# Ternary FFN on eight cores: five w2 tiles loaded ahead of the last blocks of the second product's input

## The chip, the cores and the metric

One Trainium2 chip, eight cores on two dies (cores 0 to 3, cores 4 to 7). Each core computes one eighth of the rows (half of one batch entry, 2048 of 4096 positions) of the same program, on its own data and with the same weights. The time is that of the slowest core, in microseconds (us) on the device. The kernel before took 2494.3 us as the median of three runs (2493.86, 2494.3 and 2610.59).

## The reference, cut to what matters

```python
x = _layernorm(x + attention(x, Wq, Wk, Wv, Wo))          # linear attention, 16 heads, 4 kv heads
# FFN with ternary weights:
def absmean_quant(w):
    scale = jnp.mean(jnp.abs(w))
    mask = (jnp.abs(w) >= scale * 0.7).astype(w.dtype)
    return jnp.sign(w) * mask                             # -1, 0 or 1
h = jnp.einsum('bsd,fd->bsf', x, absmean_quant(w1)) + b1  # 2048 -> 8192
h = jax.nn.gelu(h)
out = jnp.einsum('bsf,df->bsd', h, absmean_quant(w2)) + b2  # 8192 -> 2048
x = _layernorm(x + out)
```

x is (4, 4096, 2048) in f32, w1 is (8192, 2048), w2 is (2048, 8192). Both thresholds need the mean of the whole weight matrix before its first element can be made ternary.

## The kernel before, in words

Each core runs, in this order: keys, values and the small key-value matrices for a batch entry; queries and the attention output; the output projection with the first layer norm; the first FFN product (lines 742 to 828; the input in two halves P of 1024 rows, 64 steps u = 2j + P, each giving two blocks of 128 hidden features; from u = 4 each by seven block products in place of eight, Strassen's way); and the second FFN product (lines 830 to 874).

**The change to the second product** is the place of this case. The hidden activations h are bf16. They are written by ScalarE after the gelu (`store_hid`, line 1241) to a DRAM buffer `hd` in pieces of 256 KB, since on-chip memory has no room for them beside the first product's operands. For the second product they are read back by the SyncE queue (SP): `load_hid(P, half, a, b, signal)`, lines 409 to 412. P says which 1024 rows, half which 512 of them, a to b which of the 64 feature blocks (128 KB each). What is waited for before a piece may be loaded is the store of its last blocks (`d_hs`), and the end of the products or evictions that still use the memory under it.

The second product has passes: s is which 1024 rows, g which 512 of the 2048 output columns, and P (this loop's own name for the half) which 512 rows. In a pass TensorE goes through 16 weight tiles q of 2048 x 128 elements, 16 matmuls of 128x512 for each tile (4 blocks fc = 4q + j by 4 row chunks cc), 256 in all (line 856). Pass (s 0, g 0, P 0) is called the first pass below, (s 0, g 0, P 1) the second pass. The first one uses half 0 of the input, the second one half 1, with the same 16 weight tiles.

**The weight tiles** of w2 come in f32, 1024 KB each, into one of three stages, by `load_w2(r)`, lines 452 to 462, r = 16g + q. VectorE makes each ternary in two instructions (lines 960 and 963, `tern_w2` and `ternary`) and writes it as fp8, so that TensorE may use it (line 837 waits for `v_w2`). Tiles 0 to 6 of g 0 are made during the first product, and kept in MB (`W2_PRE = 7`). From tile 7 on the three stages are used in turn (MA's first half, MA's second half, MC), so the load of tile r waits for the ternary tile r - 3 to be done: `e.wait_ge(v_w2, r - 2)`, line 456. GpSimd stores each ternary tile to DRAM (`store_w2`, line 589, 256 KB), from where the second 1024 rows read it.

**What sets the order here** is the SP program, written out by hand: SP waits for semaphores in its order, and a DMA behind a wait isn't issued before that wait is over. The DMAs that SP has issued run on its own hardware queue (q1 on the page); ScalarE's (`store_hid`, and `load_x1r` for the residual) run on q10, GpSimd's on q0, all on the same 16 DMA engines. At the change of products SP does, in lines 472 to 492: load tiles 7 and 8; load half 0 blocks 0 to 12, 12 to 36; tile 9; blocks 36 to 60; wait until the stores of the other 1024 rows have landed (`d_hs[2]`, `d_hs[3]`, lines 482 and 483), since blocks 60 to 64 overwrite the memory from which they are sent; blocks 60 to 64; wait for the last eviction and gelu of the first product and for the stores of half 1; then four times a tile and 16 blocks of half 1; then the other tiles. TensorE waits for half 0 at q 0, 3, 9 and 15 (line 840), and for half 1 at q 0, 4, 8 and 12 of the second pass (line 842).

After a pass VectorE adds each of the four PSUM banks to a piece of the residual (line 1098), and GpSimd stores it.

Of the kernel before, what the change touches and what calls it, by code (L numbers as in the profile page):

```python
# [80 lines left out]
W2_PRE = 7  # L81


def build_nc():
# [191 lines left out]
    def hid_rows(a, b, half):  # L276
        base, o = (r1, (24576 + a * 512) if a < 12 else (a - 12) * 512 if a < 60 else 30720) if half == 0 else (
            (rw, a * 512) if a < 32 else (r3, 16384 + (a - 32) * 512))
        return base[:, o:o + (b - a) * 512]
# [50 lines left out]
    def n_m(u, i):  # L330
        return 7 * (u - NU_CL) + i
# [16 lines left out]
    def n_hs(j):  # L348
        return 16 * (j + 1)
# [3 lines left out]
    def n_qs(j, i):  # L353
        return 5 * (j - NU_CL // 2) + i
# [28 lines left out]
    def w2_stage(r):  # L383
        if r < W2_PRE:
            return w2_slot7
        j = (r - W2_PRE) % 3
        return maf[:, j * 2048:(j + 1) * 2048] if j < 2 else mcf[:, 0:2048]

    def w2_signal(r):
        return d_s7 if r < W2_PRE else (d_st[0], d_st[1], d_mc)[(r - W2_PRE) % 3]  # L390
# [12 lines left out]
    def sync_program(e):  # L403
# [5 lines left out]
        def load_hid(P, half, a, b, signal):  # L409
            e.wait_ge(d_hs[2 * P + half], n_hs((b - 1) // 2))  # L410
            e.dma_start(out=hid_rows(a, b, half),
                        in_=hd[P, half, :, a * 512:b * 512]).then_inc(signal, 16)
# [39 lines left out]
        def load_w2(r):  # L452
            if r == 0:
                e.wait_ge(d_x1[2], 16 * 5)
            elif r < W2_PRE or r >= W2_PRE + 3:
                e.wait_ge(v_w2, r if r < W2_PRE else r - 2)
            elif r < W2_PRE + 2:
                e.wait_ge(v_w1, 63 + r - W2_PRE)
            else:
                e.wait_ge(t_m, n_m(63, M3))  # L460
                e.wait_ge(p_q, n_qs(31, Q2))
            e.dma_start(out=w2_stage(r), in_=w2h[r // 16, r % 16]).then_inc(w2_signal(r), 16)
# [16 lines left out]
        e.wait_ge(t_m, n_m(63, M3))  # L479
        load_w2(W2_PRE + 2)  # L480
        load_hid(0, 0, 36, 60, d_ha[2])
        e.wait_ge(d_hs[2], n_hs(31))
        e.wait_ge(d_hs[3], n_hs(31))
        load_hid(0, 0, 60, 64, d_ha[3])
# [1 line left out]
        e.wait_ge(a_h, n_h(63, H22))  # L486
        e.wait_ge(d_hs[1], n_hs(31))
        for i in range(4):
            load_w2(W2_PRE + 3 + i)
            load_hid(0, 1, 16 * i, 16 * i + 16, d_hb[i])  # L490
        for r in range(W2_PRE + 7, 64):
            load_w2(r)

        e.wait_ge(t_z, 28)
# [839 lines left out]
    with nc.Block() as block:  # L1334
        block.sync(sync_program)
        block.gpsimd(gpsimd_program)
        block.vector(vector_program)
        block.scalar(scalar_program)
        block.tensor(tensor_program)
# [57 lines left out]
```

## Time and profile before

| | us |
|---|---|
| median of three runs | 2494.3 |
| the profiled execution | 2497.7 |
| its span on the slowest core (core 6) | 2496.2 |
| the spans of all eight cores | 2480.4 to 2496.2 |
| TensorE busy in that span | 2406.0 (96%) |
| VectorE, ScalarE, GpSimd busy | 1246.5, 725.6, 551.4 |
| chain that ended last: TensorE / DMA / VectorE | 87% / 10% / 2% |

How to read it: the page's busy share of TensorE says how much is left over all. Where the rest is can be read from a table of stretches with the granted clock (1.00 is the full 2.4 GHz) and from the idle times before TensorE's groups. A queue's rows (SPq) have the time at which a DMA was issued, and a DMA's landing is read from the listing of issues, which gives the time from issue to landing.

### The profile page before, as it was taken

The page shows a single profiled execution, that of the slowest core. Times are in us where ns is not written, and L with a number is a line of the kernel's source. Part 1 is how long each engine was busy: PE and PEld are TensorE (multiplying, and loading weights), DVE is VectorE, ACT ScalarE, POOL GpSimd, SP SyncE. Part 2 cuts the span into 40 slices and gives each one's busy share as a digit, 9 for nine tenths or more (in the row PEclk, how much of TensorE's full clock was granted, in tenths as well). Part 3 has the DMA queues.
Part 4 walks back from the last instruction along what each step waited for, and adds up shares of the span by engine and source line. Part 5 has one row for each costly group of instructions (what it writes and reads, how often), then busy time and mean ns, then how long its engine had stood idle before and what let it go on. Part 6 is the DMA issues. An engine that isn't in the chain of part 4 may idle for free.

```text
span 2496.2 us, 31950 instructions; the slowest of 8 cores (2480.4 to 2496.2 us)
## 1 busy us (share of the span) xinstructions
PE 2406.0 (96%) x11300; PEld 1094.4 (44%) x11300; DVE 1246.5 (50%) x1395; ACT 725.6 (29%) x1109; POOL 551.4 (22%) x419
## 2 busy tenths in 40 slices
PE   4999999999999999999999999799999999799997
PEld 1444444444444444444444444344444444344443
DVE  1222344445567777777788886375747211200021
ACT  0233477743323666666433333000000000000000
POOL 3000000004336334344343433011212000100000
PEclk9999999999999999999999999899999999899999
DMA  9994688696655887787544446976848577522253
GB/s 159 217 239 153 157 203 204 165 268 241 232 223 181 265 263 254 258 265 265 188 144 165 160 144 234 327 243 216 277 151 287 180 254 238 173 68 68 85 194 118
DMA packets 106955, 507.01 MB, mean 203 GB/s; under 512 B 12976, under 2 KB 12976, under 8 KB 69808
## 3 DMA queue, kind: packets, MB, share of 16 engines
q1 hardware_dynamic: 50400, 323.55, 38.9%
q0 software_dynamic: 27600, 124.80, 19.1%
q10 hardware_dynamic: 28800, 56.64, 7.3%
q8 instruction: 93, 1.52, 0.2%
q14 instruction: 62, 0.51, 0.1%
HBM read 444.11 MB, written 98.57 MB: 217 GB/s over the span
## 4 chain that ended last, share of the span: by engine, by line
PE 87%; DMA 10%; DVE 2%; issue 1%; POOL 0%; ACT 0%; SPq 0%; DVEq 0%; POOLq 0%; ACTq 0%
PE PB L767 29%; PE PB L856 25%; PE PB L694 8%; PE PB L731 8%; PE PB L870 4%; PE PB L668 4%; PE PB L658 4%; PE PB L758 2%; DMA MA<-w2h 2%; DMA out<-MA 2%; DMA R<-woh 2%; DMA RW<-wvh 2%; DMA zs<-MC 1%; DMA MC<-x1s 1%; DMA hd<-R 1%
## 5 line engine op out<-in xcount | busy, mean ns | idle before, releaser
L856 PE MATMUL PB<-R 128*128 128x512 fp8e4 x2576 | 572.2, 385 | 34.2 <-DVE MC L1098 17.9
L767 PE MATMUL PB<-R,RW 128*128 128x512 bf16 x2400 | 537.6, 379 | 0.0
L856 PEld LDWEIGHTS PB<-R 128*128 128x128 bf16 x2576 | 254.6, 99 | 350.5 <-issue 55.4
L767 PEld LDWEIGHTS PB<-R,RW 128*128 128x128 fp8e4 x2400 | 234.7, 98 | 283.0
L579 POOL TENSOR_TENSOR RW<-MC 128x1024 fp8e4<-128x1024 fp8e4 x120 | 244.1, 2066 | 283.1 <-DVE MC L963 283.1
L1098 DVE TENSOR_TENSOR MC<-PB,MC 128x512 f32<-128x512 f32 x56 | 38.4, 685 | 404.6 <-PE PB L856 243.9
L694 PE MATMUL PB<-R,MB 128*128 128x512 bf16 x1024 | 231.1, 379 | 0.0
L767 PE MATMUL PB<-R,MC 128*128 128x512 bf16 x960 | 226.8, 379 | 0.0
L856 PE MATMUL PB<-R,RW 128*128 128x512 fp8e4 x784 | 170.4, 379 | 0.0
L960 DVE TENSOR_SCALAR MB<-MA,thr 128x2048 fp8e4<-128x2048 f32 x102 | 137.8, 1351 | 54.6 <-DMA MA<-w2h 40.9
L963 DVE SCALAR_TENSOR_TENSOR MC<-MA,thr,MB 128x2048 fp8e4<-128x2048 f32 x64 | 158.3, 2473 | 7.0 <-DVE MB L960 0.5
L694 PEld LDWEIGHTS PB<-R,MB 128*128 128x128 bf16 x1024 | 100.1, 98 | 120.7
L658 PE MATMUL PB<-RW,R 128*128 128x512 bf16 x512 | 121.2, 390 | 28.1 <-DMA R<-xb 28.1
L1225 ACT ACT_TABLE_LOAD x1 | 1.3, 1283 | 503.1 <-DVE mv L1106 503.1
L767 PEld LDWEIGHTS PB<-R,MC 128*128 128x128 fp8e4 x960 | 93.9, 98 | 113.3
L597 POOL DMA_DIRECT2D zs<-MC x56 | 35.3, 630 | 448.9 <-DVE MC L1098 446.1
L1153 ACT ACTIVATE MA<-MA 128x2048 f32<-128x2048 f32 x69 | 130.8, 1895 | 9.8 <-DMA MA<-w1h 9.7
L1272 ACT ACTIVATE RW<-PB 128x512 f32<-128x512 f32 x180 | 105.2, 594 | 90.2 <-PE PB L767 88.3
L1324 ACT ACTIVATE lnv<-mv,c_eps_ln 128x1 f32<-128x1 f32 x8 | 2.4, 294 | 424.1 <-DVE mv L1142 416.9
L668 PE MATMUL PB<-RW,R 128*128 128x512 bf16 x512 | 119.5, 387 | 5.8 <-DMA RW<-wvh 5.8
L1253 ACT ACTIVATE R<-RW,b_sb 128x512 bf16<-128x512 f32 x120 | 85.8, 719 | 129.6 <-DVE RW L1083 62.9
L1253 ACT ACTIVATE RW<-RW,b_sb 128x512 bf16<-128x512 f32 x120 | 86.0, 720 | 127.6 <-DVE RW L1083 64.8
(134 smaller groups left out, 2525.6 us busy)
## 6 DMA issues: line engine op xcount, KB each, us to landing
MA<-w1h SPq DMA_DIRECT2D x126, 1024.0 KB, 6.5
MB<-w2h SPq DMA_DIRECT2D x108, 512.0 KB, 7.8
MA<-w2h SPq DMA_DIRECT2D x45, 1024.0 KB, 7.8
MC<-w2h SPq DMA_DIRECT2D x19, 1024.0 KB, 7.8
R<-xb POOLq DMA_DIRECT2D x32, 512.0 KB, 78.5
x1s<-R POOLq DMA_DIRECT2D x16, 1024.0 KB, 4.6
hd<-RW ACTq DMA_DIRECT2D x64, 256.0 KB, 4.6
hd<-R ACTq DMA_DIRECT2D x64, 256.0 KB, 4.9
```

Of the source, the lines that this page charges most:

```text
L579: e.tensor_tensor(w_sum(j, k), x, y, op, saturate=False).then_inc(p_q)
L658: ins = e.matmul(PB[sc % 2], xs(blk % 4, dc)[:, cc * 128:(cc + 1) * 128], wk_sb(dc), start=(dc == 0), stop=(dc == 15))
L668: ins = e.matmul(PB[2 + sc % 2], xs(blk % 4, dc)[:, cc * 128:(cc + 1) * 128], wv_sb(dc), start=(dc == 0), stop=(dc == 15))
L694: ins = e.matmul(PB[n % 3], wq_sb(ic)[:, dc * 128:(dc + 1) * 128], x_own(t, dc), start=(dc == 0), stop=(dc == 15))
L731: ins = e.matmul(PB[WO_BANK[i % 4]], attn_chunk(c, ic), wo_sb(ic, g), start=(ic == 0), stop=(ic == 15))
L767: ins = e.matmul(PB[m_bank(u, i)], w[:, dc * 128:(dc + 1) * 128], x[:, dc * 512:(dc + 1) * 512], start=(dc == 0), stop=(dc == 7))
L856: ins = e.matmul(PB[F2_BANK[P][cc]], hid(fc, P)[:, cc * 128:(cc + 1) * 128], w2q_sb(s, g, q)[:, j * 512:(j + 1) * 512], start=(fc == 0), s ...
L960: e.tensor_single_scalar(b8t, src, thr[:, 2 * no:2 * no + 1], ALU.is_le, saturate=False).then_inc(v_b)
L963: e.scalar_tensor_tensor(dst, src, thr[:, 2 * no + 1:2 * no + 2], b8t, ALU.is_ge, ALU.subtract, saturate=False).then_inc(signal)
L1153: e.activation(stage(j), stage(j), AF.Abs, accum_out=wsum[:, i:i + 1]).then_inc(a_abs)
L1253: e.activation(hb(P, half, par), src, AF.Gelu, bias=b1_sb[:, 2 * j + par:2 * j + par + 1]).then_inc(a_h)
L1272: e.activation(tq(u, slot), PB[m_bank(u, i)], AF.Copy).then_inc(a_c)
```

## The change

SP's order in the change of products. Tiles 10 to 14 are issued right behind blocks 36 to 60 of half 0, ahead of the waits for the stores and of blocks 60 to 64. Then blocks 60 to 64, and then four times 16 blocks of half 1 and a tile (15 to 18), the blocks ahead of the tile. Tiles 19 to 63 are as before. No other engine's program is changed, nor any wait on another engine.

```diff
@@ -479,6 +479,9 @@
         e.wait_ge(t_m, n_m(63, M3))
         load_w2(W2_PRE + 2)
         load_hid(0, 0, 36, 60, d_ha[2])
+
+        for r in range(W2_PRE + 3, 15):
+            load_w2(r)
         e.wait_ge(d_hs[2], n_hs(31))
         e.wait_ge(d_hs[3], n_hs(31))
         load_hid(0, 0, 60, 64, d_ha[3])
@@ -486,9 +489,9 @@
         e.wait_ge(a_h, n_h(63, H22))
         e.wait_ge(d_hs[1], n_hs(31))
         for i in range(4):
-            load_w2(W2_PRE + 3 + i)
             load_hid(0, 1, 16 * i, 16 * i + 16, d_hb[i])
-        for r in range(W2_PRE + 7, 64):
+            load_w2(15 + i)
+        for r in range(19, 64):
             load_w2(r)
```

The SP queue at this place, from blocks 36 to 60 of half 0 (the first row, 128x12288) to the third piece of half 1. `w2h` are the f32 weights, `hd` the hidden activations; 128x2048 from `hd` is blocks 60 to 64, 128x8192 is 16 blocks of half 1.

```order
 L411 DMA R<-hd 128x12288
+L462 DMA MA<-w2h 128x2048 x2
+L462 DMA MC<-w2h 128x2048
+L462 DMA MA<-w2h 128x2048 x2
 L411 DMA R<-hd 128x2048
-L462 DMA MA<-w2h 128x2048
+L411 DMA RW<-hd 128x8192
+L462 DMA MC<-w2h 128x2048
 L411 DMA RW<-hd 128x8192
 L462 DMA MA<-w2h 128x2048
-L411 DMA RW<-hd 128x8192
-L462 DMA MC<-w2h 128x2048
```

Five tile loads (10 to 14) now stand ahead of the short piece of half 0. Tile 15 (into MC) has now blocks 60 to 64 and one piece of half 1 ahead of it; it had all four pieces of half 1 and tiles 10 to 14 ahead of it before.

## Rows read from the trace of the kernel before

**Rows 1.** Stretches of core 6: engines' busy us (instructions), clock, DMA share, GB/s.
```profile
1550.00:1633.10 83.10, 66.85 (x258) 27.30 (x257) 34.28 (x21) 1.54 (x3) 6.07 (x9) 0.84 0.96 315
1633.10:2019.00 385.90, 385.90 (x1790) 174.94 (x1789) 211.33 (x152) 0.00 (x0) 63.81 (x76) 1.00 0.69 224
```

**Rows 2.** TensorE in order of time: start, us, what, idle before and releaser.
```profile
1550.05 24.34 PE L856 MATMUL PB<-MB,R 128*128 128x512 fp8e4 x112
1574.22 13.98 PE L856 MATMUL PB<-R 128*128 128x512 fp8e4 x64
1592.28 6.50 PE L856 MATMUL PB<-R 128*128 128x512 fp8e4 x16 [4.08 <-DVE R L963]
...
1613.17 6.30 PE L856 MATMUL PB<-R 128*128 128x512 fp8e4 x16 [3.91 <-DVE R L963]
1623.53 9.70 PE L856 MATMUL PB<-R 128*128 128x512 fp8e4 x32 [4.05 <-DVE R L963]
1633.06 24.34 PE L856 MATMUL PB<-MB,RW 128*128 128x512 fp8e4 x112
```

**Rows 3.** VectorE in order of time: second instruction of tiles 7, 9, 10 and 11.
```profile
1552.91 2.35 DVE L963 SCALAR_TENSOR_TENSOR R<-MA,thr,MB 128x2048 fp8e4<-128x2048 f32 x1
...
1560.61 2.35 DVE L963 SCALAR_TENSOR_TENSOR R<-MC,thr,MB 128x2048 fp8e4<-128x2048 f32 x1
...
1580.30 2.35 DVE L963 SCALAR_TENSOR_TENSOR R<-MA,thr,MB 128x2048 fp8e4<-128x2048 f32 x1
...
1589.79 2.35 DVE L963 SCALAR_TENSOR_TENSOR R<-MA,thr,MB 128x2048 fp8e4<-128x2048 f32 x1
```

**Rows 4.** The SP queue in order of time (issues).
```profile
1550.83 20.50 SPq L411 DMA_DIRECT2D R<-hd  x2
1571.59 0.61 SPq L462 DMA_DIRECT2D MA<-w2h  x1
1572.30 0.43 SPq L411 DMA_DIRECT2D RW<-hd  x1
...
1592.21 0.33 SPq L462 DMA_DIRECT2D MA<-w2h  x1
```

**Rows 5.** The SP queue's own waits, 1500 to 1665: total, times, longest.
```profile
SPq L483 <- DMA hd<-R: 12.9, 1, 12.9
```

**Rows 6.** Single issues: KB, us to landing. Issued 1550.39, 1550.83, 1571.59, 1572.30, 1592.21.
```profile
MC<-w2h SPq DMA_DIRECT2D x1, 1024.0 KB, 7.7
R<-hd SPq DMA_DIRECT2D x1, 3072.0 KB, 19.9
MA<-w2h SPq DMA_DIRECT2D x1, 1024.0 KB, 7.2
RW<-hd SPq DMA_DIRECT2D x1, 2048.0 KB, 13.2
MA<-w2h SPq DMA_DIRECT2D x1, 1024.0 KB, 27.3
```

**Rows 7.** Two short stretches of the first pass (columns of rows 1).
```profile
1585.00:1590.00 5.00, 3.20 (x15) 1.26 (x13) 1.50 (x2) 0.00 (x0) 0.00 (x0) 1.00 1.00 369
1590.00:1600.00 10.00, 6.50 (x16) 2.15 (x16) 3.03 (x2) 0.00 (x0) 0.54 (x1) 0.66 1.03 340
```

**Rows 8.** TensorE behind a wait of 3 us: core 6, then core 1 (x208 each).
```profile
776.81 46.13 PE L758 MATMUL PB<-R,MC 128*128 128x512 bf16 x208
769.43 45.06 PE L758 MATMUL PB<-R,MC 128*128 128x512 bf16 x208
```

**Rows 9.** All TensorE waits of core 6: total, times, longest.
```profile
PE PB L856 <- DVE MC L1098: 17.9, 4, 10.8
PE PB L856 <- DVE R L963: 16.2, 4, 4.2
```

**Rows 10.** Spans and clocks of the two slowest cores.
```profile
core 0: 2491.5 us, clock 0.989
...
core 6: 2496.2 us, clock 0.987
```

## The prediction, made before the changed kernel ran

> **What bounds the kernel now.** I read the stretches first: around the change of products TensorE's clock is at a mean of 0.84 and TensorE is busy 66.85 of 83.1 us, while the next 386 us are busy throughout at 1.00 [rows 1]. So the whole of what this edit can touch is in the first pass of the second product. TensorE in order of time gives the size: the first pass starts at 1550.05 and the second at 1633.06, 83.0 us apart. 112 matmuls without a gap take 1574.22 - 1550.05 = 24.17 us from start to start, 0.2158 each, so 256 would take 55.25 [rows 2]. The pass loses 27.8 us. The same rows say how: the tiles up to 10 come in time, and each of tiles 11 to 14 is waited for by about 4 us, released by the second ternary instruction. The four waits are 16.2 us in all [rows 9]. Behind each the 16 matmuls take 6.3 to 6.5 us in place of 3.62 (three times, about 8.2 us) and the last 32 take 9.70 in place of 7.07 (2.6) [rows 2]: they run in part at 1.2 GHz, mean clock 0.66 in the ten microseconds behind the first wait [rows 7]. 16.2 + 8.2 + 2.6 = 27.0; the other 0.8 is starting up again.
>
> What is late is the transfer. VectorE needs 3.8 us for a tile (1552.91 to 1560.61 for two tiles [rows 3]), but tile 10 is only ready at 1582.65 and tile 11 at 1592.14. Tile 10's stage was free at 1555.26, when tile 7 was done [rows 3]; its load was issued at 1571.59 [rows 4], since SP stood in front of it for the last of the activation stores, 12.9 us of it on one wait [rows 5]. From there tiles and pieces of half 1 alternate, so each tile carries 2048 KB that nobody needs before the second pass. The issue-to-landing rows give the rate: half 1's first piece lands at 1572.30 + 13.2 = 1585.5, tile 14 at 1592.21 + 27.3 = 1619.5, and between these lie 10 MiB (tiles 11 to 14 and three pieces), 3.40 us for one MiB [rows 6].
>
> **The change, step by step** (times of core 6).
>
> 1. *Blocks 36 to 60* are issued and land as before: 1550.83 + 19.9 = 1570.7 [rows 6]. TensorE wants them at tile 9, at 1550.05 + 9 x 3.45 = 1581.1. The new loads stand behind them in the same queue.
>
> 2. *Tiles 10, 11, 12* are issued at 1555.3, 1559.1 and 1563.0, when tiles 7, 8 and 9 are done [rows 3]. They run behind the piece, by the rate above landing at 1574.1, 1577.5 and 1580.9. Made ternary with 3.8 us each: ready at 1577.9, 1581.7, 1585.5. TensorE would start tile 11 at 1550.05 + 11 x 3.453 = 1588.0 and tile 12 at 1591.5.
>
> 3. *Tiles 13 and 14* are issued when 10 and 11 are ready, 1577.9 and 1581.7. The queue still has work then. They land at about 1584.3 and at 1588 to 1589 (the latter by 7.2 us from issue, as tile 10 had [rows 6]), ready at 1589.3 and 1592.8; wanted at 1594.9 and 1598.4. All four waits of today go, 27.8 us with their slow matmuls.
>
> 4. *What is late next* is tile 15. In front of it now stand blocks 60 to 64 (0.5 MiB) and half 1's first piece (2 MiB). SP issues these behind load 14 at 1582 (the stores that it waits for had landed by 1570.9 before), and tile 15 when tile 12 is done, 1585.5. From 1570.7 on the queue has to move 5 tiles, 0.5 and 2 MiB and tile 15: 8.5 MiB at 3.40 = 28.9 us, so it lands at 1599.6, and is ready at 1603.4 + 0.1 for the handover. It is wanted at 1550.05 + 15 x 3.453 = 1601.85. That is a wait of 1.6 us. The rate may move either way: it was taken beside four stores of ternary tiles in 34 us, and now five or six fall into 25 us, which takes some of it; the engines moved 340 to 369 GB/s in all at this time [rows 7], and with 45 GB/s for the stores 295 to 325 GB/s are left, 3.55 to 3.23 us for one MiB, a wait of 0.2 to 2.9. I take 2.
>
> 5. *The clock behind that wait.* Nothing before shows a wait of 2 us here. The lower bound is nothing, as after a wait of 3 us on core 1 (208 matmuls in 45.06), the upper the 2.8 us that followed the waits of 4 us [rows 2]. The same 3 us on core 6 cost 46.13 - 45.06 = 1.07 in that row [rows 8]. I take 1.1, the nearest.
>
> 6. *Half 1 comes later*: its first piece at 1570.7 + 7.5 x 3.40 = 1596.2 in place of 1585.5. The second pass would start at 1550.05 + 55.25 + 3.1 = 1608.4, and wants one piece every 13.8 us. The others land behind tiles 15, 16 and 17, one every 10.2 us: about 1606, 1617 and 1627, against 1622, 1636 and 1650. Cost nothing, with a cover of 12 us or more. If that cover goes, each microsecond counts in full.
>
> 7. *Tiles 16 to 18* now land at 1610, 1620 and 1630, each behind a piece. They are wanted from 1608.4 + 55.25 = 1663.6 on, and from 19 on the loads go by the stages as before. Cost nothing; the cover is 30 us. SP's five moved issues cost 0.3 to 0.6 us each [rows 4] in time that it spent waiting. GpSimd's stores of ternary tiles follow the tiles and nobody waits for them here.
>
> Sum: -27.8 + 2.0 + 1.1 = -24.7 us. Everything behind the second pass is paced by TensorE or follows it, so it moves along. The profiled execution took 2497.7, so it would take 2473.0; the median of the runs is 3.4 lower, 2494.3, and gives 2469.6, **2470 us**. Core 6 is slowest by 4.7 us over core 0 [rows 10]; the edit takes about the same from each, so I let it stay.
>
> At step 4 a page speaks against my wait. The rate in the rows is 1048576 / 3.40 = 308 GB/s for SP's queue, and 340 and 369 for all queues. The Trainium skill's page "DMA: Bandwidth & Descriptors" (Specifications) gives about 358 GB/s as one core's share of HBM. An estimate from that page: 8.9 MB would take 24.9 us if SP's queue had all of it, tile 15 would land at 1595.6 and TensorE would not wait at all; the sum would be -27.8. The two rows lie on both sides of the page's figure, and they hold stores too.
>
> **The rivals.**
>
> *No wait at tile 15* (chance 0.18). If the queue moves one MiB in under 3.2 us, tile 15 is ready in time. The first piece of half 1 took 1585.5 - 1578.8 = 6.7 us for 2 MiB behind tile 10 [rows 6], 3.35 for one, which speaks for a rate near the edge. Time: 2494.3 - 27.8 = 2466.5. That is also where the page's figure above would put it.
>
> *Tile 15 much later* (0.16). Between tile 9's landing (1550.39 + 7.7 = 1558.1) and 1570.7 the queue needed 12.6 us for 3 MiB, 4.2 for one [rows 6], with the activation stores and the residual's loads beside it. At that rate 8.5 MiB take 35.7, tile 15 is ready at 1610.3, the wait is 8.4, and 2.8 go to the clock: -16.6, 2477.7. Against it: those stores and loads are over by then.
>
> *The gain is partly given back later* (0.06). Core 6 waits 17.9 us on evictions in the second half of the kernel [rows 9]. This follows from DMAs that start when TensorE ends its first 1024 rows, so it should only move; but a shift could change it by some 5 us either way: 2465 to 2475, or up to 2480 together with a later tile 15.
>
> *Slower than before* (0.02). Half 1's pieces, put behind five tiles, come too late for the second pass. It decides from 1608 on: the first piece would have to land after 1608.4 before anything is lost, and after 1633 before all the gain is. It has 2494.3 + (landing - 1633) as its time, 2497 if it lands at 1636. That would be 65 us for 7.5 MiB, 8.7 for one, twice the worst rate in the rows. SP's wait for the stores of half 1 could hold it up so, but the longest such wait was 12.9 us [rows 5].
>
> That leaves 0.58 for the forecast with gains of 22 to 27 (2467 to 2472). The low end is the first rival with 2.5 us for the scatter of the cores, 2464. The high end takes in the late tile 15 with some given back later, 2481. A change of 2% is 50 us (about what a measurement of this kernel tells from none), and the whole of what the first pass loses is 27.8. So within 2% has 0.97, faster 0.01, slower 0.02 for what no row shows.
>
> **What would show it.** In the changed kernel's trace: no wait of TensorE on the ternary instruction at tiles 11 to 14; the first pass 55 to 61 us long in place of 83.0; one wait of 0 to 4 us ahead of its last 16 matmuls; the tile loads of 10, 11 and 12 issued 3.8 us apart ahead of 1565; the first piece of half 1 landing ahead of the second pass; the clock over the first pass at 0.95 or more. It is wrong if tiles 11 to 14 are still waited for (the loads in front are slower than I read), if the second pass waits for half 1, or if the first pass is 25 us shorter and the span is not.

## The result, and the profile after

The changed kernel took 2474.35 us (median of four runs, 2472.83 to 2476.28). Its ratio to the kernel before is 0.9922, 95% interval 0.9902 to 0.9941: 19.5 us less of 2494.1. In some executions a whole die is disturbed and slower (two of the four now on record for the kernel before, 2610.59 and 2820.3); all ratios, and the medians below, leave these out. The forecast was 2470 and 24.7 us less. The profiled execution took 2473.52 us, its slowest core is core 6 again, with 2472.0 us in place of 2496.2; as a mean over the eight cores the span went from 2486.1 to 2467.0 us, 19.0 less. Run again on another chip it gave 0.9933 (0.9916 to 0.9950).

The stretches of core 6 of the changed kernel around the first pass, with the columns of [rows 1]:

```profile
1547.40:1612.90 65.50, 58.25 (x259) 25.66 (x257) 34.29 (x21) 1.55 (x3) 7.59 (x9) 0.92 0.99 307
1612.90:1990.00 377.10, 377.10 (x1749) 171.00 (x1748) 211.29 (x152) 0.00 (x0) 63.28 (x76) 1.00 0.74 243
```

TensorE of core 6 in order of time, the answer to [rows 2]:

```profile
1547.46 24.34 PE L859 MATMUL PB<-MB,R 128*128 128x512 fp8e4 x112
1571.63 27.79 PE L859 MATMUL PB<-R 128*128 128x512 fp8e4 x128
1606.67 6.36 PE L859 MATMUL PB<-R 128*128 128x512 fp8e4 x16 [7.25 <-DVE R L966]
1612.87 24.34 PE L859 MATMUL PB<-MB,RW 128*128 128x512 fp8e4 x112
```

The four waits at tiles 11 to 14 are gone: 112 + 128 matmuls run without a gap. One wait is there, 7.25 us ahead of the last 16 matmuls, and these take 6.36 us, 2.74 more than the 3.62 at 2.4 GHz: the mean clock of the pass is 0.92, and was 0.84. The first pass is 65.4 us long in place of 83.0. Over the eight cores its mean went from 81.6 to 64.2, and that is 17.5 us.

VectorE of core 6, the first ternary instruction of tiles 10, 11, 14 and 15; the SP queue; and the landing of the load of tile 15, issued at 1584.99 (answers to [rows 3, 4, 6]):

```profile
1573.13 1.29 DVE L963 TENSOR_SCALAR MB<-MA,thr 128x2048 fp8e4<-128x2048 f32 x1 [12.76 <-DMA MA<-w2h]
1577.32 1.29 DVE L963 TENSOR_SCALAR MB<-MA,thr 128x2048 fp8e4<-128x2048 f32 x1 [0.45 <-DMA MA<-w2h]
...
1588.87 1.29 DVE L963 TENSOR_SCALAR MB<-MA,thr 128x2048 fp8e4<-128x2048 f32 x1
1602.67 1.29 DVE L963 TENSOR_SCALAR MB<-MC,thr 128x2048 fp8e4<-128x2048 f32 x1 [10.06 <-DMA MC<-w2h]
```

```profile
1552.74 4.18 SPq L462 DMA_DIRECT2D MA<-w2h  x2
1560.44 0.33 SPq L462 DMA_DIRECT2D MC<-w2h  x1
1576.94 4.52 SPq L462 DMA_DIRECT2D MA<-w2h  x2
```

```profile
MC<-w2h SPq DMA_DIRECT2D x1, 1024.0 KB, 17.5
```

Tiles 10 to 14 come at the pace of VectorE, 3.85 us apart (4.19 between the first two, with 0.45 of waiting). Then it idles 10.06 us for tile 15, which landed at 1584.99 + 17.5 = 1602.5, 55.0 us after the pass began. The forecast had it at 49.55.

The TensorE waits of core 6, with [rows 9] as the lines of before:

```profile
PE PB L859 <- DVE MC L1101: 13.8, 2, 11.6
PE PB L859 <- DVE R L966: 7.2, 1, 7.2
```

Core 6's span is 24.2 us shorter, and that is 17.6 in the first pass, 4.1 less wait between the halves of the rows (17.9 to 13.8), and 2.6 by a first pass that began at 1547.46 in place of 1550.05. The last two are within the scatter of the cores and runs: over the eight cores the wait between the halves is a mean of 15.4 us before, 13.9 after, and 14.6 in the changed kernel run again, and the first pass begins 0.2 us earlier as a mean. So it is luck that core 6's 24.2 us come so near to the 24.7 of the forecast; the edit's own part is 17.5.

### The profile page after: what moved, and what is told of

The parts are those of the page before. It is cut to its first block, busy times and chain, and to the rows that moved or that the text cites. A ratio compares the mean times of both kernels' runs of the same rounds, so it can differ in the third digit from the quotient of the medians.

```text
span 2472.0 us, 31808 instructions; the slowest of 8 cores (2462.5 to 2472.0 us)
## 1 busy us (share of the span) xinstructions
PE 2388.4 (97%) x11158; PEld 1092.8 (44%) x11300; DVE 1246.5 (50%) x1395; ACT 725.9 (29%) x1109; POOL 553.9 (22%) x419
## 4 chain that ended last, share of the span: by engine, by line
PE 85%; DMA 10%; DVE 3%; issue 2%; POOL 1%; DVEq 0%; ACT 0%; POOLq 0%; ACTq 0%; SPq 0%
PE PB L770 29%; PE PB L859 25%; PE PB L697 8%; PE PB L734 7%; PE PB L873 4%; PE PB L661 4%; PE PB L671 4%; PE PB L761 2%; DMA R<-woh 2%; DMA RW<-wvh 2%; DMA out<-MA 1%; DMA zs<-MC 1%; DMA MA<-w2h 1%; DMA MC<-x1s 1%; DMA MA<-zs 1%
## 5 line engine op out<-in xcount | busy, mean ns | idle before, releaser
L859 PE MATMUL PB<-R 128*128 128x512 fp8e4 x2576 | 563.7, 382 | 21.1 <-DVE MC L1101 13.8
```

The source lines that it names most:

```text
L859: ins = e.matmul(PB[F2_BANK[P][cc]], hid(fc, P)[:, cc * 128:(cc + 1) * 128], w2q_sb(s, g, q)[:, j * 512:(j + 1) * 512], start=(fc == 0), s ...
```

## The experiments

What was open: why tile 15 is 5.4 us later than worked out, and where the cover of 12 and 30 us that steps 6 and 7 counted on stands. In the comparisons "start" is VectorE's first instruction of a tile, from the beginning of the first pass, as a mean over the eight cores. The changed kernel has tile 10 at 24.9 and tile 15 at 54.4, and in its repeat 25.5 and 54.9. "Mean span" is the mean over the eight cores and the runs, against the kernel before run beside it; the changed kernel's repeat has 17.4 us less.

**Tile 15 ahead of its piece.**

```diff
         for i in range(4):
-            load_hid(0, 1, 16 * i, 16 * i + 16, d_hb[i])
             load_w2(15 + i)
+            load_hid(0, 1, 16 * i, 16 * i + 16, d_hb[i])
```

> The changed kernel, but each of tiles 15 to 18 is issued ahead of its piece of half 1 and not behind it, so that only blocks 60 to 64 stand ahead of tile 15; tiles 10 to 14 stay early. In the changed kernel tile 15 landed 55.1 us after the first pass began, and the 2 MiB piece ahead of it took 8.1 us of the queue. Theory Q (tile 15 is late because of the bytes ahead of it in SP's queue): tile 15 is issued at 37.5, lands at 47 to 48, is ready at 51 to 52, wanted at 51.8: wait 0 to 0.5 us, first pass 55.3 to 56, second pass starts with a wait of 0 to 1 us for its first piece, which now lands at 55.4; 9 to 10 us faster than the changed kernel, about 0.988 of the kernel before (2465). Rival P (the piece is what the second pass can't spare): the second pass waits for pieces, 3 us or more, and under half of the 10 us stays. Rival W (tile 15 is late because SP waits for the store semaphores or for a stage): tile 15 still lands after 52, wait over 4 us.

Measured: tile 15's start is 47.4, the pass 55.2 to 57.3 us (mean 56.0, 8.1 less than in the changed kernel), the second pass waits 0.3 us for a piece on one core and nothing on the others. But the kernel has 0.9911 of before (0.9887 to 0.9935), median 2468.46: beside the 0.9922 of the changed kernel that is some 3 us and not 9 to 10, though both intervals are 5 us wide to either side. The mean span is 23.8 us less than before, so the mean core did get about 6 of the 8.1 us; the slowest core, which sets the time, did not. TensorE on core 2, which was the slowest:

```profile
1542.47 24.34 PE L859 MATMUL PB<-MB,R 128*128 128x512 fp8e4 x112
1566.64 27.79 PE L859 MATMUL PB<-R 128*128 128x512 fp8e4 x128
1595.61 3.61 PE L859 MATMUL PB<-R 128*128 128x512 fp8e4 x16 [1.17 <-DVE R L966]
...
1701.52 11.86 PE L859 MATMUL PB<-R 128*128 128x512 fp8e4 x48 [5.45 <-DVE R L966]
```

So theory Q holds for the first pass, P and W fall. And there is a wait that was not foreseen: 5.45 us at 1701.5, tile 12 of the third pass (the first with new weight tiles). All eight cores together give a mean of 2.0 us of such waits (0 to 5.9), which is about what the mean span lacks of the 8.1. VectorE shows why:

```profile
1600.15 0.67 DVE L1101 TENSOR_TENSOR MC<-PB,MC 128x512 f32<-128x512 f32 x1
...
1624.48 0.69 DVE L1101 TENSOR_TENSOR MC<-PB,MC 128x512 f32<-128x512 f32 x1 [22.85 <-DMA MC<-x1s]
...
1629.64 0.69 DVE L1101 TENSOR_TENSOR MC<-PB,MC 128x512 f32<-128x512 f32 x1 [3.67 <-DMA MC<-x1s]
...
1694.19 0.69 DVE L1101 TENSOR_TENSOR MC<-PB,MC 128x512 f32<-128x512 f32 x1 [10.56 <-DMA MC<-x1s]
```

Behind the first pass it stands 22.85 and 3.67 us in front of the residual for evictions 2 and 3, and only then makes tile 16; behind the second pass 10.56 us more, with tile 28 (tile 12 of the third pass) next in its program. Tile 16 starts 85.4 us after the first pass began, as a mean, and 89.8 in the changed kernel: VectorE's chain moved by 4.4 us where TensorE's moved by 8.1.

**The stores of the ternary tiles 7 to 15 held until tile 15 is ternary** (changed kernel otherwise; GpSimd's program).

```diff
         for q in range(16):
+            if q == 7:
+                e.wait_ge(v_w2, 16)
             store_w2(0, q)
```

> The changed kernel, but GpSimd stores the ternary tiles 7 to 15 only when tile 15 is ternary, so that none of these 256 KB stores runs beside SP's queue in the last 34 us before tile 15. Nothing is left out. In that stretch SP's queue had 82% of the DMA engines' time and the stores 11.5% (before: 92.6% and 7.4% in the stretch from which the rate of 3.40 us for one MiB was taken). Theory S (the stores share the engines): SP's share goes to 93%, the rate from 3.97 to about 3.5 us for one MiB, tile 15 lands at 51 to 52 us from the start of the first pass in place of 55.2, the wait falls from 7.25 to 3 to 4 us and the pass from 65.4 to about 61.5; time about 0.9905 of before. Rival C (the limit is the memory that all cores share, reads above all, and not the engines' time): SP's queue gets nothing, tile 15 lands at 54 to 56, wait 6.5 to 8. If deferring the stores costs something later (tile 16 may not be written before tile 7 to 15's stores have landed), it is seen as waits at tile 16, expected none.

Measured: tile 15's start is 49.2 (46.4 to 51.9) in place of 54.4, and tile 10's 23.3 in place of 24.9. Three cores have no wait at tile 15 at all, the others 1.1 to 4.0; the mean pass is 58.1 us. Rival C falls: SP's queue does get what the stores leave. The DMA queues of core 6 between the starts of tiles 10 and 15, the changed kernel first (29.5 us), then this one (24.8 us):

```profile
q1 hardware_dynamic: 988, 7.96, 84.4%
q0 software_dynamic: 400, 1.31, 11.0%
q10 hardware_dynamic: 117, 0.20, 3.0%
```

```profile
q1 hardware_dynamic: 996, 8.09, 96.1%
q10 hardware_dynamic: 118, 0.21, 3.2%
```

For about the same 8 MB SP's queue (q1) needed 29.5 us with 84.4% of the engines' time and 24.8 us with 96.1%: 269 and 326 GB/s, or 3.89 and 3.21 us for one MiB. The share alone makes 29.5 into 25.9 us (times 84.4 over 96.1). The other 1.1 us is that SP's own bytes took the engines 6% less time each without the stores beside them; why, no run here tells.

The time, 0.9920 of before (0.9897 to 0.9942), is that of the changed kernel all the same, and so is the mean span, 17.8 us less. On all cores TensorE now waits in the third pass from tile 12 on, 2.3 to 5.8 us in all (mean 4.1, of 6.0 won in the first pass). The expectation had none of that. Part of it is of the experiment's own making: GpSimd issues the nine held stores right ahead of the store of eviction 0, and VectorE stands 25.2 to 29.1 us in front of eviction 2, 18.3 to 20.1 in the changed kernel. Core 6:

```profile
1565.38 31.24 PE L861 MATMUL PB<-R 128*128 128x512 fp8e4 x144
...
1697.94 16.49 PE L861 MATMUL PB<-R 128*128 128x512 fp8e4 x64 [4.63 <-DVE R L968]
```

**The first residual loads held too.** In `load_x1r`, for the first one, `e.wait_ge(v_w2, 16)` on ScalarE's queue is added to the kernel above.

> As e2_stores_late, and the first loads of the residual (ScalarE's queue, 256 KB each, 2 KB packets) are also held until tile 15 is ternary. Theory S: another 5% of the engines' time for SP, tile 15 lands at 49 to 50.5 us from the start of the first pass, wait 1 to 2.5 us, pass about 59. Blocks 36 to 60 should also land a little earlier than 21.4. Rival C: no change against e2_stores_late. The evictions behind the first pass come later (about 20 us), which nobody should wait for.

Measured: tile 10 starts at 21.6, tile 15 at 47.3, the pass is 55.9 us as a mean: another 1.9 us, as theory S has it. The wait at tile 12 of the third pass is 4.0 to 13.0 us, on all cores, a mean of 7.0 of the 8.3 that the first pass won, and the one run took 2473.66 us.

**Pieces of half 1 ahead of the tiles alone**, in the kernel before.

```diff
         for i in range(4):
-            load_w2(W2_PRE + 3 + i)
             load_hid(0, 1, 16 * i, 16 * i + 16, d_hb[i])
+            load_w2(W2_PRE + 3 + i)
```

> The kernel before with one part of the change alone: each of the four pieces of half 1 is issued ahead of the tile with which it alternates (10 to 13), and no tile is moved up. Theory Q (bytes ahead in SP's queue set when a tile is there): tile 10 lands at about 36 us from the start of the first pass in place of 28.8, and each tile up to 13 about 7 us later than before, tile 14 and 15 by about nothing to 4; a new wait at tile 10 (wanted at 34.5, ready at 40), and the pass 83 to 88 us, so 0 to 5 us slower than before: 2494 to 2499. Rival: the order within the pairs makes no difference, pass 83 as before, no wait at tile 10.

Measured: tile 10 starts at 34.7 in place of 27.7, the 7 us of one piece, and is waited for on core 6 (5.49 us). The pass is 81.2 us as a mean, before 81.6; one run took 2487.96 us beside a kernel before of 2489.6. The order in the queue does what theory Q says, but the new wait at tile 10 takes the place of another: the queue has the same bytes to move until tile 14. I had expected up to 5 us more. By itself this half of the change brings nothing that one run can show, and within the change it costs the first pass 8 us (the first experiment).

**VectorE's order of evictions and tiles**, with tile 15 ahead of its piece. In each pass of the first 1024 rows three ternary tiles are put between the first two and the last two evictions; GpSimd's stores are put in the same order.

```diff
-        for c in range(4):
-            evict_z(0, 0, c)
         for g in range(4):
+            for c in range(2):
+                evict_z(0, g, c)
             if g < 3:
-                for q in range(12):
+                for q in range(3):
                     tern_w2(g + 1, q)
-            for c in range(4, 8):
+            for c in range(2, 4):
+                evict_z(0, g, c)
+            ...                     # tiles 3 to 11
+            for c in range(4, 6):
                 evict_z(0, g, c)
+            ...                     # tiles 12 to 14, evictions 6 and 7, tile 15
```

> e1_tile15_first, and VectorE (with GpSimd's stores in the same order) no longer waits idle for the residual between evictions 2 and 3 of a pass: three ternary tiles stand between the first two and the last two evictions of each pass of the first 1024 rows. In e1_tile15_first the eight cores waited up to 7 us in all (0 to 5.4 at once, about 152 us after the first pass began, which is tile 12 of the third pass), since VectorE had stood 17 to 26 us in front of two residual loads and then began tile 16 late. Theory G (the gain of a shorter first pass is given back there, because VectorE's chain of tiles 16 to 31 does not move with TensorE): these waits fall to 0 to 1 us, the mean over cores to under 0.3, all else as e1_tile15_first; about 0.9885 of the kernel before. Rival N (e1_tile15_first was held by other things, such as the evictions between the two halves of the rows or the spread between runs): the waits at 152 us go and the time stays at 0.991. Rival T (tiles 16 to 18 land late behind the pieces of half 1, so that moving them up in VectorE's order gives nothing): waits at 150 to 170 us stay.

Measured: 0.9887 of the kernel before (0.9871 to 0.9902), median 2462.68 us. The slowest core of the profiled run has 2461.1 us. The waits in the third pass are 0.55 and 0.90 us on two cores and none on the others, a mean of 0.18 in place of 2.0; the second pass starts with a wait of 0.3 and 0.8 us on two cores. This is theory G, and T falls. Against N stand the mean span, 26.5 us less than before, which is 9.1 less than the change on the same chip and about what its shorter first pass (55.8 for 64.4) gives, and the ratio beside the 0.9911 of the first experiment. That kernel ran on another chip, and the two intervals overlap, so how much the new order alone brings is not shown.

On VectorE of core 4, which was that slowest one, evictions 1 and 2 (line 1108, counted from 0) have now three tiles between them, and there is no wait for the residual:

```profile
1601.01 0.67 DVE L1108 TENSOR_TENSOR MC<-PB,MC 128x512 f32<-128x512 f32 x1
...
1606.49 1.29 DVE L970 TENSOR_SCALAR MB<-MA,thr 128x2048 fp8e4<-128x2048 f32 x1 [4.01 <-DMA w2qd<-R]
...
1618.73 1.29 DVE L970 TENSOR_SCALAR MB<-MA,thr 128x2048 fp8e4<-128x2048 f32 x1 [8.50 <-DMA MA<-w2h]
...
1632.05 1.28 DVE L970 TENSOR_SCALAR MB<-MC,thr 128x2048 fp8e4<-128x2048 f32 x1 [9.58 <-DMA MC<-w2h]
...
1635.71 0.68 DVE L1108 TENSOR_TENSOR MC<-PB,MC 128x512 f32<-128x512 f32 x1
```

It is the fastest kernel of this study; the change has 0.9933 on the same chip.

**The same order of VectorE with the change's order of SP.**

> The changed kernel with VectorE's and GpSimd's order of e5_tile15_first_evict_split alone; SP's order is the change's. The changed kernel has no wait at tile 12 of the third pass. Theory G: it is the cover that was used up, not yet a wait, so nothing moves: first pass 62 to 66 us as in the changed kernel with one wait at tile 15, time within 0.1% of the changed kernel beside it. Rival: the evictions or their order matter in themselves (in later passes, or between the halves), and it is 0.2% or more off.

Measured: 0.9925 (0.9909 to 0.9941), the change beside it 0.9933 (0.9916 to 0.9950); one wait at tile 15, 3.1 to 9.2 us, none in the third pass; the mean span is 18.1 us less than before, the change's 17.4. As expected: by itself the order of VectorE brings nothing that can be told here, since the change has no wait in the third pass.

**Half 1 in pieces of 4 blocks**, four DMAs in place of one, so rows of 4 KB and not of 16 KB.

> The changed kernel, each 16-block piece of half 1 loaded as four DMAs of 4 blocks, so that a row that the queue moves for them has 4 KB in place of 16 KB; same bytes, same place. Theory R (the 16 engines take turns between the queues row by row, so that a 256 KB transfer with 2 KB rows is held up by long rows beside it): the residual loads behind the first pass land faster, VectorE's wait of 18 us for evictions 2 and 3 falls to 8 to 12, and tile 15 comes later (the stores get a larger part), wait at tile 15 8 to 12 us in place of 7.25. Rival F (the share follows bytes, whatever the rows are): both stay as in the changed kernel, 18 us and 7.25 on the slowest core.

Measured: one run, 2475.38 us. VectorE's wait for evictions 2 and 3 is 17.6 us as a mean, in the changed kernel run beside it 20.2; tile 15's start 55.5 against 54.9, the wait there 7.6 against 7.0. Both move the way that theory R says, but by less than half of what it asked for, and the wait at tile 15 by less than the cores of one run differ. Row length is at best a small part; how the engines share their time between queues stays open.

**The change again.**

> The changed kernel itself, to have it beside e5 and e6 on the same chip. All theories: 0.992 of the kernel before, one wait of 4 to 9 us at tile 15 in the first pass, none at tile 12 of the third.

Measured: 0.9933, a wait of 4.1 to 9.5 us at tile 15, none in the third pass.

## Why the prediction was right in kind and off in size

The time, 2474.35, is in the range (2464 to 2481), and the four waits went as told. The gain is 19.5 us and not 24.7, and the step that failed is step 4. Step by step:

- *The size of the loss* (83.0 us for a pass of 55.25) and what made it, SP standing in front of the activation stores, then 2048 KB ahead of each tile: right. With the tiles issued early they come at VectorE's pace. The bytes ahead of a tile set when it lands, as the first and the fourth experiment show by taking away and adding one piece: 7 us each for tile 15 and tile 10.
- *Steps 1 to 3*: right but for small delays: blocks 36 to 60 landed 21.4 us after the pass began (forecast 20.7), tile 10 at 25.7 (24.1), tile 13 was ready at 41.3 (39.3), tile 14 at 45.2 (42.8). They are 0.7 to 2.4 us late, each more than the one before, and none was late for TensorE.
- *Step 4, the mis-sized term*: a wait of 2.0 us at tile 15 was forecast, 7.25 measured on core 6 and 6.5 as a mean. From the landing of blocks 36 to 60 to that of tile 15 the queue took 33.7 us for 8.5 MiB, 3.97 for one and not 3.40. The rate came from a stretch in which SP's queue had 92.6% of the engines' time; in the changed kernel it had 82.1%. The queues of core 6 from 1568.8 to 1602.5 in the changed kernel, then from 1585.5 to 1619.5 in the kernel before (packets, MB, share of the 16 engines' time):

```profile
q1 hardware_dynamic: 1106, 8.78, 82.1%
q0 software_dynamic: 482, 1.57, 11.5%
q10 hardware_dynamic: 233, 0.41, 5.3%
```

```profile
q1 hardware_dynamic: 1018, 10.57, 92.6%
q0 software_dynamic: 301, 1.03, 7.4%
```

  The share alone makes 28.9 us into 32.6, and SP's bytes taking a little more engine time each makes the rest. What had taken the share is on two queues: GpSimd's stores had 11.5% (7.4% in the other stretch), and ScalarE's queue, with the end of the activation stores and two residual loads, 5.3% (nothing in the other). I had put in 45 GB/s for the stores (my own five or six in 25 us would have been 52 to 63), and they moved 47; I had put in nothing for ScalarE's queue, writing that its transfers are over by then; and I had let all queues together move 340 to 369 GB/s, from two short stretches, where they moved 320. With the nine stores away tile 15 came 5.2 us earlier, 3.21 us for one MiB between tiles 10 and 15; with the residual loads away too, 1.9 more. Together that is 7.1 us, more than the whole 5.4 that were missed. The rival for a later tile 15 (8.4 us of wait, 16 in 100) gave 2477.7; the measurement lies between it and the forecast.
- *The page's figure*: with the Trainium skill's 358 GB/s from "DMA: Bandwidth & Descriptors" (Specifications) the wait would have been none. In this stretch SP's queue moved 260 GB/s and all queues 320; between tiles 10 and 15 with the stores away they moved 326 and 335. As a bound on such a stretch the page's figure is not contradicted (the 369 of [rows 7] are five microseconds); as the rate of SP's queue, which is how the estimate used it, the trace does not agree. The rival without a wait (0.18) rested on the same: it asked for one MiB in under 3.2 us.
- *Step 5, the clock*: 1.1 us forecast, 2.74 measured. In these runs the eleven waits of 0.4 to 1.9 us at tile 15 cost 0.1 to 0.6 us beyond themselves, two of 2.1 and 2.4 us cost 1.85 each, and those of 3.1 us and more 1.5 to 3.1. The row for the wait that came was that of the 4 us waits, which belongs to the longer wait of step 4. And "nothing before shows a wait of 2 us" held for core 6 alone. Tile 11 of the kernel before on cores 1 and 7:

```profile
1582.17 5.30 PE L856 MATMUL PB<-R 128*128 128x512 fp8e4 x16 [2.43 <-DVE R L963]
1584.40 3.61 PE L856 MATMUL PB<-R 128*128 128x512 fp8e4 x16 [2.69 <-DVE R L963]
```

  Behind the wait of 2.4 us the 16 matmuls took 1.7 us more than 3.6, and behind that of 2.7 us no more: these rows give the term for a wait of 2 us no single value.
- *Step 6*: right. No core of the changed kernel waited for half 1; on core 6 the first piece landed at 1599.3, 13.6 us ahead of the second pass.
- *Step 7*: no wait, but the cover was misread. I counted 30 us for tile 16. What decides is tile 28, which VectorE makes behind four evictions of the first pass and four of the second, with waits for residual loads among them: 18.3 and 8.4 us on core 6. The second of these, and the first instruction of tile 28:

```profile
1696.86 0.69 DVE L1101 TENSOR_TENSOR MC<-PB,MC 128x512 f32<-128x512 f32 x1 [8.38 <-DMA MC<-x1s]
...
1699.65 1.27 DVE L963 TENSOR_SCALAR MB<-MA,thr 128x2048 fp8e4<-128x2048 f32 x1
```

  The tile was ready at 1703.4 and wanted at 1709.6, a cover of 6 us. The first, second and third experiment took 6 to 8 us off the first pass, and got waits there of 2.0, 4.1 and 7.0 us as a mean.
- *Given back later* (0.06): this was put between the halves of the rows, where nothing changed beyond scatter. In the change itself it did not come; in the first three experiments it did in part, at a place that the forecast had not named.
- *The signs*: no wait at tiles 11 to 14 and the early issues came as told. The first pass of 65.4 us (55 to 61 said), the wait of 7.25 (0 to 4) and the clock of 0.92 (0.95 or more) did not, and all three follow from step 4.
- *The chances*: within 2% is what happened. But it was said once that 2% is what a measurement tells from none, and that is wrong for this kernel. The interval of the ratio is 0.2% wide to either side, and 0.8% is clear of it. The change is a gain that can be told. The text had a sign of it: the times 2493.86, 2494.3 and 2497.7 that stand ahead of the prediction lie within 0.2%, and 24.7 us is 1%.

## What to carry to other kernels

A transfer rate read from one stretch holds for the mix of that stretch. When an edit moves loads into another stretch, count for that stretch what every other queue still has to move, the ones that are late included. When a stall is shortened, follow the engine that feeds the next stage through its whole program order up to the first thing it delivers late: the cover is the smallest one on that way, not the first. Look at the slowest core and at the mean of all: a wait that costs the mean core 2 us can cost the slowest one 5. And put long transfers that nobody needs yet behind the one short transfer that is next.

## What the runs showed of the hardware

The stores on GpSimd's queue cost SP's queue a little more than the bytes they moved. Between tiles 10 and 15 of core 6 they were 1.31 of 9.50 MB. Given to SP's queue, these would be 16% more for it; without them it moved 21% more in a microsecond (326 for 269 GB/s), and the engines as a whole moved 335 GB/s in place of 321. Why, no run here tells.

Small transfers take long beside a full SP queue. Between evictions 1 and 2 of the first pass a 256 KB store on GpSimd's queue and a 256 KB load on ScalarE's stand one behind the other. In the changed kernel, with the pieces of half 1 still on their way, VectorE waited 18.3 to 20.1 us for the two (on core 6 the store took 9.7 us from issue to landing, and the load 9.9); in the kernel before, where these pieces had landed by then, 4.3 to 7.6 (2.6 and 3.5). With the long rows of SP's queue cut to a quarter the wait for evictions 2 and 3 changed by 2.6 of 20.2 us, so what holds the small transfers up stays open.
